# First attention: value products in pairs of steps, projections beside them in four 32-column tiles, maxima dealt by the matrix engine's time

## The reference, cut to what matters

```python
q = (x @ Wq).reshape(b, t, H, D).transpose(0, 2, 1, 3)
ckv = x @ Wkva
kv_latent, k_rope = (ckv[:, :, :R], ckv[:, :, R:])
kv = (kv_latent @ Wkvb).reshape(b, t, H, NOPE).transpose(0, 2, 1, 3)
q = jnp.concatenate([q_nope, _rope(q_rope)], axis=-1)
k = jnp.concatenate([kv, _rope(k_rope)], axis=-1)
v = jnp.concatenate([kv, jnp.zeros_like(k_rope)], axis=-1)
att = jnp.einsum('bhqd,bhkd->bhqk', q, k) / jnp.sqrt(jnp.float32(D))
att = jnp.where(mask, att, jnp.float32(-jnp.inf))
att = jax.nn.softmax(att, axis=-1)
y = jnp.einsum('bhqk,bhkd->bhqd', att, v)
return y.transpose(0, 2, 1, 3).reshape(b, t, H * D) @ Wo
```

## Time and profile before

| | |
|---|---|
| median of 3 runs | 2065.22 us (2065.14 to 2065.44) |
| profiled execution, first to last instruction | 2053.3 us, so 11.9 us of the median lie around it |
| TensorE busy over the span | 1796.1 us (87%) |
| VectorE, ScalarE, GpSimd busy | 1482.7, 1106.1, 645.5 us |
| first attention, first scores to last | 225.25 to 999.7 us |

### The profile page before, as it was taken

How to read it: one execution, slowest core, us unless ns; L and a number is a source line. 1 busy time by engine, 2 the same in 40 slices (tenths; PEclk the granted TensorE clock), 3 DMA queues, 4 the chain that set the end, 5 groups by cost and what they waited for, 6 DMA issues and landing times. The chain is left out here.

```text
span 2053.3 us, 32652 instructions
## 1 busy us (share of the span) xinstructions
PE 1796.1 (87%) x12065; PEld 646.5 (31%) x12065; DVE 1482.7 (72%) x3109; ACT 1106.1 (54%) x1385; POOL 645.5 (31%) x776
## 2 busy tenths in 40 slices
PE   6547899999999999999789988888888888889798
PEld 3115333333333333333333341211211211112465
DVE  5875766666666766665354589999999999995643
ACT  4402245454444444445333238888887888887432
POOL 0031544554454454442141402402501320001154
PEclk9768999999999999999989989999999999999898
DMA  4000000000000000000130201221211221211114
GB/s 132 0 0 1 1 12 25 24 30 23 23 23 23 23 23 23 23 23 34 27 115 11 103 1 37 79 80 50 78 64 59 79 74 58 76 59 35 62 31 144
DMA packets 56266, 91.62 MB, mean 45 GB/s; under 512 B 21652, under 2 KB 30164, under 8 KB 55980
## 3 DMA queue, kind: packets, MB, share of 16 engines
q1 hardware_dynamic: 54540, 85.86, 12.1%
q0 software_dynamic: 1280, 2.62, 0.5%
q10 hardware_dynamic: 288, 1.05, 0.2%
HBM read 46.15 MB, written 38.51 MB: 41 GB/s over the span
## 5 line engine op out<-in xcount | busy, mean ns | idle before, releaser
L1760 DVE TENSOR_REDUCE h_m_half<-h_ps_max 128x1 f32<-128x512 f32 x1024 | 635.8, 682 | 32.1 <-PE h_ps_max L1367 29.4
L1616 ACT ACTIVATE h_P<-h_ps_st 128x1024 f32<-128x1024 f32 x512 | 497.8, 1023 | 86.0 <-PE h_ps_st L1383 83.4
L998 ACT ACTIVATE l_P<-l_ps_st 128x1024 f32<-128x1024 f32 (+3 forms) x384 | 306.9, 809 | 288.3 <-PE l_ps_st L846 287.3
L846 PE MATMUL l_ps_st<-l_Q,l_K 64*128 64x512 f32 (+3 forms) x1536 | 327.8, 506 | 2.5 <-DMA l_Q<-l_m_row 2.5
L1087 DVE CUSTOM_DVE_ANT_0 l_masked<-l_ps_t,l_mask 128x384 bf16<-128x384 f32 (+3 forms) x512 | 230.2, 487 | 82.3 <-PE l_ps_t L804 80.8
L1393 PE MATMUL h_ps_o<-h_P,h_V 128*9 128x512 f32 x2048 | 267.7, 595 | 0.7 <-ACT h_P L1616 0.5
L1367 PE MATMUL h_ps_max<-h_K,h_Q 48*128 48x512 bf16 x1024 | 201.0, 389 | 66.9 <-DVE h_m_half L1760 64.8
L1090 DVE TENSOR_REDUCE l_m_half<-l_ps_t 128x1 f32<-128x512 f32 x256 | 164.8, 686 | 95.3 <-PE l_ps_t L804 95.1
L1047 POOL TENSOR_SCALAR_AFFINE_SELECT l_P<-l_P 128x256 f32<-128x256 f32 x256 | 103.3, 409 | 375.5 <-ACT l_P L998 375.0
L1383 PE MATMUL h_ps_st<-h_Q,h_K 51*128 51x512 bf16 x1024 | 167.3, 379 | 14.4 <-ACT h_P L1616 10.3
L1367 PEld LDWEIGHTS h_ps_max<-h_K,h_Q 48*128 48x128 bf16 x1024 | 49.2, 93 | 387.2 <-DVE h_m_half L1760 372.8
(11 more groups left out here) (452 smaller groups left out, 2235.9 us busy)
## 6 DMA issues: line engine op xcount, KB each, us to landing
sums<-l_o SPq DMA_DIRECT2D x15, 512.0 KB, 2.6
sums<-h_o SPq DMA_DIRECT2D x15, 512.0 KB, 2.6
h_K<-k_parts SPq DMA_DIRECT2D x32, 192.0 KB
h_Q<-q_parts SPq DMA_DIRECT2D x32, 192.0 KB
y_rows<-zero SPq DMA_DIRECT2D x8, 512.0 KB, 4.9
c_W<-c_W SPq DMA_DIRECT2D x32, 128.0 KB, 2.1
c_W<-in_W SPq DMA_DIRECT2D x16, 256.0 KB, 4.0
c_back<-y_rows SPq DMA_DIRECT2D x16, 256.0 KB, 5.4
```

The source lines that it names most:

```text
L846: last = pe.matmul(ps_st[x % 2][:, a, 0:w], K[n // NG % 2][rows, kt * 128:(kt + 1) * 128], Q[n % NQ][rows, c, p, q0 - c * CH:q0 - c * CH + ...
L998: act.activation(P[e % PR][:, :, 0:w], ps_st[slot["s", n, i, p] % 2][:, :, 0:w], ACT.Exp, scale=0.125).then_inc(consumed, 1)
L1616: act.activation(P[e % PR][:, :, :], ps_st[x % 2][:, :, :], ACT.Exp, scale=1.0 / 12.0).then_inc(consumed, 1)
L1760: dve.tensor_reduce(m_half[:, half, 2 * p + a, qt:qt + 1], ps_max[:, t % NB, :], AX.X, ALU.max, negate=True)\
```

## The change

- The value products come in pairs: in every even step those of the two steps before (`products`), so that they follow one another without scores between. `P` gets six buffers in place of four (`PR`); the two new ones lie on weights that are read only while the folded weights are made (`W.early`).
- Projections of queries and keys and the output products are made as four products of 32 columns each instead of one of 128, and stand directly behind the pair of value products (`beside_units`). The latent values stay as they are.
- The units of the maxima are dealt by `give` in proportion to TensorE's time: after the first scores, after the second, and behind the products of even steps, with no upper limit on how many follow one another.
- The turns of the maxima move: that of the second half to step 0 (from step 2), that of the first half to step 8 (from step 9), both behind the products (`turns_behind`). On SP, `place_maxima(2n+1)` moves ahead of `fetch_sums(n-1)`; on VectorE `invert` moves from a quarter to a third of a phase's units.

```diff
--- before.py
+++ after.py
@@ -561,8 +561,9 @@
     W = S.latent = State()
     W.Wq, W.Wk, W.Wl, W.Wvo = sb("Wq", [D, H, 64]), sb("Wk", [D, 128]), sb("Wl", [D, 16]), sb("Wvo", [128, 3, D])
     W.cos, W.sin, W.one_row, W.mask = sb("cos", [128, T]), sb("sin", [128, T]), sb("one_row", [128, 1]), sb("mask", [128, CH])
-    W.sums, W.WkvbP = sb("sums", [128, 128]), sb("WkvbP", [128, NG, 64])
-    W.WqnT, W.WkvbD, W.Wo = sb("WqnT", [128, NG, D]), sb("WkvbD", [128, NG, D]), sb("Wo", [128, NG, D])
+    W.sums, W.early = sb("sums", [128, 128]), sb("early", [128, 4 * NG * D])
+    W.WqnT, W.WkvbD, W.Wo = [W.early[:, k * NG * D:(k + 1) * NG * D].rearrange("p (g d) -> p g d", g=NG) for k in range(3)]
+    W.WkvbP = W.early[:, 3 * NG * D:3 * NG * D + NG * 64].rearrange("p (g d) -> p g d", g=NG)
     W.loaded = semaphore(nc, ctx, "l_weights_loaded")
     W.count = 12
 
@@ -590,7 +591,7 @@
 
 
     R, M, KT, NGR = 16, 17, T // 128, B * NG
-    NQ, NOB, NB, PR, NFIRST = 3, 4, 3, 4, 6
+    NQ, NOB, NB, PR, NFIRST = 3, 4, 3, 6, 6
     STEPS = [(c, kt, max(c * CH, kt * 128), (c + 1) * CH - max(c * CH, kt * 128)) for c in range(2) for kt in range(4 * c + 4)]
     NI = len(STEPS)
     FIRST = sum(s[0] == 0 for s in STEPS)
@@ -599,9 +600,15 @@
     NORM_AT = FIRST
 
 
-    def turn_steps(n):
-
-        return {3 if n == 0 else 2: 2 * n + 1, NI - 3: 2 * n + 2} if n + 1 < NGR else {2: 2 * n + 1}
+    def turns_ahead(n, i):
+
+        return [1] if (n, i) == (0, 3) else []
+
+    def turns_behind(n, i):
+
+        if i == 0 and n:
+            return [2 * n + 1]
+        return [2 * n + 2] if i == 8 and n + 1 < NGR else []
 
 
     def key_units(b):
@@ -614,18 +621,29 @@
         return [("max", n, qt, p, lo, min(CH, (qt + 1) * 128 - lo)) for c in halves for qt in range(c * KT // 2, (c + 1) * KT // 2)
                 for p in range(2) for lo in range(0, (qt + 1) * 128, CH)]
 
-    def phase_units(n):
-        out = max_units(n + 1) if n + 1 < NGR else []
-        extra = (key_units((n + 2) // NG) if n + 2 < NGR and (n + 2) % NG == 0 else []) + (query_units(n + 2) if n + 2 < NGR else [])
-        for k, unit in enumerate(extra):
-            out.insert(min(len(out), 1 + 2 * k), unit)
-        if n % NG == 1 and n >= NG:
-            for c in range(2):
-                out.insert(len(out) - 3 + 2 * c, ("out", n // NG - 1, c))
-        return out
+    def beside_units(n):
+
+        keys = key_units((n + 2) // NG) if n + 2 < NGR and (n + 2) % NG == 0 else []
+        queries = query_units(n + 2) if n + 2 < NGR else []
+        outs = [("out", n // NG - 1, c) for c in range(2)] if n % NG == 1 and n >= NG else []
+        at = {i: [] for i in range(0, NI, 2)}
+        if keys:
+            at[0] = keys[0:2]
+            at[2] = keys[2:]
+        for k, unit in enumerate(queries):
+            at[2 * k + (4 if n == 0 else 2 if keys else 0)].append(unit)
+        for k, unit in enumerate(outs):
+            at[8 + 2 * k].append(unit)
+        return at
 
     def cost(unit):
         return {"max": unit[-1], "v": CH, "out": 2 * CH}.get(unit[0], CH) + 64
+
+    def products(n, i):
+
+        if i % 2 or n + i == 0:
+            return []
+        return [(n, i - 2), (n, i - 1)] if i else [(n - 1, NI - 2), (n - 1, NI - 1)]
 
     units = [("q", 0, p, 0) for p in range(2)] + max_units(0, (0,))
     units.insert(0, ("k", 0, 0))
@@ -637,10 +655,43 @@
     units += max_units(0, (1,))
     for k, unit in enumerate(query_units(1)):
         units.insert(SCORES_FROM + 1 + 4 * k, unit)
-    phase_from = []
+    late_units = units[SCORES_FROM:]
+    units = units[:SCORES_FROM]
+    plan, phase_from, emitted_by = {}, [], {}
+
+    def give(pool, places):
+
+        total, left, share = sum(cost(u) for u in pool), list(pool), 0
+        for key, weight in places:
+            share += weight / sum(w for _, w in places)
+            while left and sum(cost(u) for u in pool[:len(pool) - len(left)]) < share * total - 1:
+                plan[key].append(left.pop(0))
+        assert not left
+
     for n in range(NGR):
-        phase_from.append(len(units))
-        units += phase_units(n)
+        for i in range(NI):
+            for place in ("first", "second", "beside", "behind"):
+                plan[n, i, place] = []
+    give(late_units, [((0, i, place), STEPS[i][3]) for i in range(3) for place in ("first", "second", "behind")])
+    for n in range(NGR):
+        beside, places = beside_units(n), []
+        for i in range(3 if n == 0 else 0, NI):
+            w = STEPS[i][3]
+            places += [((n, i, "first"), w), ((n, i, "second"), w)]
+            if i % 2 == 0:
+                plan[n, i, "beside"] = beside[i]
+                places.append(((n, i, "behind"), sum(STEPS[x][3] for _, x in products(n, i)) + CH * len(beside[i])))
+        if n + 1 < NGR:
+            give(max_units(n + 1), places)
+    for n in range(NGR):
+        if n:
+            phase_from.append(len(units))
+        for i in range(NI):
+            if n == 0 and i == 3:
+                phase_from.append(len(units))
+            for place in ("first", "second", "beside", "behind"):
+                units += plan[n, i, place]
+            emitted_by[n * NI + i] = len(units)
     phase_from.append(len(units))
     tile_of, reduced_by, turn_of = [], {}, {}
     tiles = 0
@@ -655,19 +706,6 @@
     out_tile = {unit[1]: t for unit, t in zip(units, tile_of) if unit[0] == "out"}
 
 
-    emitted_by = {}
-    edges = [(0, 0, 2, SCORES_FROM, phase_from[0])]
-    edges += [(n, 3 if n == 0 else 1, NI if n + 1 < NGR else NI - 1, phase_from[n], phase_from[n + 1]) for n in range(NGR)]
-    for n, first, last, lo, hi in edges:
-        span = [n * NI + k for k in range(first, last + 1)]
-        weight = [STEPS[k % NI][3] + 256 for k in span]
-        total, at, share = sum(cost(u) for u in units[lo:hi]), lo, 0
-        for k, w in zip(span, weight):
-            share += w / sum(weight)
-            while at < hi and sum(cost(u) for u in units[lo:at]) < share * total - 1:
-                at += 1
-            emitted_by[k] = at
-
     def emitted(n, i):
 
         return emitted_by.get(n * NI + i, SCORES_FROM)
@@ -675,9 +713,9 @@
     order = [("turn", 0)]
     for n in range(NGR):
         for i in range(NI):
-            if i in turn_steps(n):
-                order.append(("turn", turn_steps(n)[i]))
+            order += [("turn", h) for h in turns_ahead(n, i)]
             order += [("s", n, i, p) for p in range(2)]
+            order += [("turn", h) for h in turns_behind(n, i)]
     slot = {x: k for k, x in enumerate(order)}
 
     sums0 = nc.dram_tensor("sums0", [NGR, 128, T], F32).ap()
@@ -698,7 +736,7 @@
         Kh = [sb(f"Kh{i}", [128, T], BF16) for i in range(2)]
         Kl = [sb(f"Kl{i}", [128, T], BF16) for i in range(2)]
         V = [sb(f"V{i}", [128, KT, M]) for i in range(B)]
-        P = [sb(f"P{i}", [128, 2, CH]) for i in range(PR)]
+        P = [sb(f"P{i}", [128, 2, CH]) for i in range(PR - 2)] + [W.early[:, k * 2 * CH:(k + 1) * 2 * CH].rearrange("p (a c) -> p a c", a=2) for k in range(2)]
         t1 = [sb(f"t1_{i}", [128, CH]) for i in range(2)]
         t2 = [sb(f"t2_{i}", [128, CH]) for i in range(2)]
         o = [sb(f"o{i}", [128, T]) for i in range(NOB)]
@@ -772,10 +810,9 @@
 
             place_maxima(0)
             for n in range(NGR):
+                place_maxima(2 * n + 1)
                 if n:
                     fetch_sums(n - 1)
-                place_maxima(2 * n + 1)
-                if n:
                     spread_sums(n - 1)
                 if n + 1 < NGR:
                     place_maxima(2 * n + 2)
@@ -813,17 +850,21 @@
                     c = unit[2]
                     pe.wait_ge(normed, 4 * (x + 1))
                     for g in range(2):
-                        last = pe.matmul(tile(t), Wvo[:, g, :], packed[(2 * x + g) % 3][:, c * CH:(c + 1) * CH],
-                                         start=(g == 0), stop=(g == 1))
+                        for j in range(4):
+                            last = pe.matmul(tile(t)[32 * j:32 * j + 32, :], Wvo[:, g, 32 * j:32 * j + 32], packed[(2 * x + g) % 3][:, c * CH:(c + 1) * CH],
+                                             start=(g == 0), stop=(g == 1))
                     last.then_inc(tile_ready, 1)
                 elif kind == "k":
-                    pe.matmul(tile(t), Wk[:, :], xn[:, batch(x, unit[2])], start=True, stop=True)\
-                      .then_inc(tile_ready, 1)
+                    for j in range(4):
+                        last = pe.matmul(tile(t)[32 * j:32 * j + 32, :], Wk[:, 32 * j:32 * j + 32], xn[:, batch(x, unit[2])], start=True, stop=True)
+                    last.then_inc(tile_ready, 1)
                 else:
                     _, n, p, c = unit
                     h = (n % NG) * HG + 2 * p
-                    pe.matmul(tile(t), Wq[:, h:h + 2, :].rearrange("d h r -> d (h r)"),
```

(45 more changed lines are left out.)

## The result

The changed kernel takes 2119.51 us, median of 4 runs (2119.04 to 2121.35), against 2065.33 (2065.14 to 2069.11) for the kernel before: a ratio of 1.0264, 95% interval 1.025 to 1.0279. The forecast was 2119.

What follows compares the result with a forecast made beforehand. TensorE was taken to set the pace. 48 us of saved tiling edges against 102 us of new stalls gave 54 us more: 2053.3 + 54 + 11.9 = 2119 us, range 2070 to 2145.

Steps and rivals of the forecast that it cites:

- rival A: Whole first attention: second maxima units stall on the three PSUM tiles as walked; 2119 us, own range 2095 to 2142; chance 0.72.
- B: Stalls in the attention much shorter than walked, because VectorE is busy only 64% and catches up; 2070 to 2095; chance 0.10.
- C: Saved edges decide in the attention, once new stall is under 48 us, some 3.3 a phase; 2017 us; chance 0.10.
- the walk: Place-by-place timing of TensorE and VectorE through each attention phase; for a plain phase it gave 9.2 us of stall.
- D: More waits in the attention: the sums' transfer (28 us) on top, or masks queued on GpSimd; 2147 us; chance 0.05.
- the cover of 2 us: Sums' transfer lands near 12 us into its phase, VectorE asks near 14; without this margin, 28 us more over 14 phases.
- The signs: Attention: plain phases near 50.7 us, idle near 9, maxima waits over 100, no gap before projections, value pairs 1.70 + 0.13.
- Step 6 as walked: Plain phase, projection behind two value products: the next maxima start 1.6 us late, the 384-wide unit 0.97 late.
- 48 us saved: Over the attention: fewer and shorter changes of tiling for value products, projections and output products, 3.3 us a plain phase.
- 102 lost to new stalls: Over the attention: new TensorE stalls on PSUM tiles, 102 us in sum (54 + 48).
- 6.8 us a phase: Plain phase before the change: 46.9 - 38.0 - 2.1 = 6.8 us taken as tiling edges, what the change can win.
- 11.9 us around the span: Whole program: runs take 2065.2 us, the profiled first-to-last instruction span 2053.3; the 11.9 us between were kept in the sum.

## Why the forecast was right

**The bound and the mechanism.** TensorE set the pace, its edges were saved, and more was lost to tiles. Taking the order away and leaving all else turned +53 into -20 us, so rival A's mechanism is shown, and not merely fitting. *B* (VectorE catches up in its idle time) fell: it is idle for 2.29 us ahead of the projection in step 6 and TensorE still stands 1.5 us behind it, as walked, and all stalls together are as long as forecast (below). *C* fell at its own condition: new stall of 5.3 us a phase by the record's idle time (6.1 in the walk's count) where it needed less than 3.3. *D* (the sums' transfer, masks) didn't appear: VectorE waits for the sums' transfer once, in the last phase, where it also did before (9.2 us, before 5.8), and in none of the 14 phases that had the cover of 2 us; the score products' only transfer wait is 1.6 us once, and the only wait for GpSimd's masks is the 0.6 us named above. VectorE's waits for the sums over the attention:

```profile
DVE l_flat L1170 <- DMA l_flat<-sums: 9.2, 1, 9.2
```

The Trainium skill's sentence that tiling speeds up TensorE but not the emptying of PSUM (TensorEngine Tiling (Array Packing), PSUM Bottleneck) agrees with the runs, with one thing added by them: at VectorE's same 30.3 to 30.6 us a phase the attention lasts 825.2 or 751.6 us, so the order of the emptying decides, not its sum.

**The signs.** Plain phases near 50.7 us, the projections without a gap and the pair of value products came out as named. Idle time was to be near 9 us in a plain phase and is 7.34, and the maxima's waits over 100 us and are 97.5: the record leaves out 0.16 us of each stop, eleven of them in a plain phase, and with these 1.8 us a plain phase stands for 9.1 us, where the walk had 9.2.

**Step 6 as walked.** Counted from the projection's start, the maxima were forecast at 0.98, 2.93 and 2.93 + 0.65 + 0.97 = 4.55; they start at 0.97, 2.81 and 4.42. The stall behind a projection (1.5) and that of maxima on maxima (0.96) are the rows' values.

**The phases.** Plain: 50.7 forecast, 50.21 measured. With outputs 53.2, measured 52.33. With keys 56.6, measured 55.14. Phase 0: 2 more forecast, 4.2 measured (two of the slow spots below lie in it). Phases 14 and 15: 0 forecast, -0.4 and -0.1 measured.

**What the sum had wrong, and what cancelled.** The forecast had 48 us saved and 102 lost to new stalls. Its walk counts a stall from start to start less the streaming, but for the kernel before it took the idle time of the record, which is 0.16 us less for each stop. The attention before has 91 stops of TensorE, the changed one 171. Counted as in the walk, the stalls before are 39.5 + 14.8 = 54.3 us and after 112.8 + 27.9 = 140.7; the forecast's were 39.5 + 102 = 141.5. So its new stalls were hit in their level, but the growth is 86.4 us and not 102, because those before were set too low; the same 15 us stood among the edges, "6.8 us a phase", of which 1.0 was stall. That slip enters both terms and drops out of their difference.

The edges saved are what is left of TensorE's busy time. It fell by (772.0 - 39.5) - (825.2 - 112.8) = 20.1; the 80 more stops add 13.1 of modelled ends to it, and the six slow spots described below some 1.6 each. So about 43 us were saved where the forecast had 48. Two parts of this were measured by themselves: the form of the projections is worth 0.66 a phase, where form and place together were put at 1.3, and an excursion of the values 0.25, where it was put at 0.33. Against the forecast that is 5 saved less, 16 lost less and 10 for the slow spots, which it didn't have: 54 + 5 - 16 + 10 = 53. That the total came out within a microsecond is in part luck, since slow spots that nobody had foreseen stand against growth that was set too high. The sign, the level of the stalls and the lengths of the phases are no luck.

**The rest of the program.** The forecast kept "11.9 us around the span". That step was wrongly read: the changed kernel's profiled run took 2119.95 us for a span of 2118.2, so 1.75 us lie around a span. The rest of the 11.9 fits an execution that was shorter than the median outside the attention: in the profile of the kernel before 1056.1 us lie behind it and 225.3 ahead of it, in that of the changed kernel 1064.9 and 228.2, in parts of the program that the change leaves alone. It did no harm, since the sum needed the median plus the growth of the attention, which is the same: 2065.2 + 54.

## What to carry to other kernels

Before products that feed the same few PSUM tiles are put together to save changes of tiling, write down what empties the tiles and how long it takes: each unit that followed another directly on a full set of tiles stood here until the first one was emptied, though the emptying engine was busy only 60% of the time. Put work that needs no tile (scores, values) between two such units, and the slowest to empty (a projection) ahead of the longest such work. Against the kernel before, the grouping was worth -20 to -25 us here with the consumers in a good order and +53 in a bad one, so weigh the dealing rule first.

## What the hardware showed that was not expected

- TensorE's clock fell in the attention of the changed kernel, where it had been 1.00 from end to end before. At 254.3, 274.8, 438.6, 568.3, 650.3 and 909.7 us the granted clock is 0.50 (1.2 GHz) for 3.4 us, as in the last window above. Ahead of 438.6 lies the densest place of step 6, with TensorE busy 1.66 of 3.40 us, and ahead of the others 1.27 to 1.66; its longest single wait for VectorE is 1.5 us. A plain phase with one takes 51.72 instead of 50.21. The kernel with one maxima unit to a place has two in phase 0, which is dealt as in the changed one, and none after it: there the stalls cost more than their own length. They are not the only thing that such a fall goes with. In the kernel with the keys spread the clock falls at 573.9 us with TensorE busy 3.07 of the 3.40 us before, 1.9 of them in the 16-column products of the latent values. What decides it was not tried.
- A change of tiling around float32 products of 512 columns costs 0.10 to 0.13 us each way. Products of the same tiling follow each other at 0.86 to 0.87 us, also when one writes to the value sums and the next to a tile of `ps_t`, and at 0.97 when maxima come next. Four 32-column tiles make one product of 128 columns at that same distance, and this is worth 0.17 us where value products stand ahead of it.
